# Scan stage: GpSimd also takes the product with B of step 5, eight of the 24 steps of a unit

## What is computed

```python
def _selective_scan(xs, dts, A, Bs, Cs):
    def step(h_prev, t):
        x_t, dt_t, B_t, C_t = t
        dA = jnp.exp(dt_t[..., None] * A)
        dBx = (dt_t * x_t)[..., None] * B_t[:, :, None, :]
        h = dA * h_prev + dBx
        y = jnp.einsum('bkdn,bkn->bkd', h, C_t)
        return (h, y)
    ...
    _, ys = jax.lax.scan(step, h0, seq)
```

## Time and profile before

| | before |
|---|---|
| median of 3 runs | 21461.23 us (21459.94 to 21463.92) |
| the profiled execution, its own time | 21461.03 us |
| its span, first to last instruction | 21459.2 us |
| mean granted TensorE clock | 0.785 of full speed |
| VectorE busy | 19058.9 us |
| GpSimd busy | 15280.9 us |
| TensorE matmuls busy | 16247.2 us |
| ScalarE busy | 10090.7 us |

### The profile page before, as it was taken

The page is one execution under the profiler, slowest core; times in us unless marked ns, Lnnn a source line. Parts: engine busy times, 40 slices in busy tenths (PEclk is TensorE's granted clock), DMA queues, the critical chain, the costliest instruction groups (busy, mean ns, idle before and its releaser), DMA issues. The chain is left out here.

```text
span 21459.2 us, 289980 instructions
## 1 busy us (share of the span) xinstructions
PE 16247.2 (76%) x83096; PEld 5502.1 (26%) x83096; DVE 19058.9 (89%) x21113; ACT 10090.7 (47%) x19239; POOL 15280.9 (71%) x5892
## 2 busy tenths in 40 slices
PE   8999999999977777777777777777777777777731
PEld 5555555522211111111111111111111111111111
DVE  5555555589989999999999999999999999999966
ACT  4444444467754444444444444444444444444410
POOL 0000000056669999999999999999999999999977
PEclk9999999989987777777777777777777777777755
DMA  1000000056666666666666666666666666666666
GB/s 22 18 18 18 18 18 18 18 195 226 229 196 129 127 134 131 128 132 130 129 134 131 127 132 132 129 131 131 128 133 133 127 130 133 130 131 133 127 147 166
DMA packets 1129481, 2520.46 MB, mean 117 GB/s; under 512 B 247606, under 2 KB 448824, under 8 KB 1112960
## 3 DMA queue, kind: packets, MB, share of 16 engines
q1 hardware_dynamic: 1128320, 2508.11, 52.3%
HBM read 2000.43 MB, written 507.38 MB: 117 GB/s over the span
## 5 line engine op out<-in xcount | busy, mean ns | idle before, releaser
L1235 POOL TENSOR_TENSOR c_pr<-c_hs,c_c_u 128x1568 f32<-128x1568 f32 x3072 | 9934.9, 3238 | 1037.5 <-DVE c_hs L1199 762.2
L1133 ACT ACTIVATE c_psum<-c_dt_u,c_a_neg 128x784 f32<-128x784 f32 x6144 | 5641.7, 918 | 7475.1 <-DVE c_hs L1199 7422.3
L1199 DVE TENSOR_TENSOR_SCAN c_hs<-c_psum,c_dbx 128x785 f32<-128x785 f32 (+1 forms) x4352 | 7616.3, 1773 | 20.2 <-issue 20.2
L1065 PE MATMUL c_psum<-c_pr,c_red 128*64 128x392 f32 x24576 | 7211.0, 705 | 1.0 <-POOL c_pr L1235 1.0
L1054 PE MATMUL c_psum<-c_br_u,c_sel 48*128 48x512 bf16 (+1 forms) x8704 | 2965.6, 433 | 4029.9 <-DVE c_dbx L1176 3927.8
L1176 DVE TENSOR_TENSOR c_dbx<-c_u_u,c_psum 128x784 f32<-128x784 f32 x4352 | 4103.1, 943 | 40.0 <-PE c_psum L1054 40.0
L1224 POOL TENSOR_TENSOR c_dbp<-c_u_u,c_bp_u 128x784 f32<-128x784 f32 x1792 | 3316.1, 1850 | 105.2 <-DVE c_hs L1199 62.6
L1199 DVE TENSOR_TENSOR_SCAN c_hs<-c_psum,c_dbp 128x785 f32<-128x785 f32 (+1 forms) x1792 | 3191.5, 1781 | 0.0
L196 POOL TENSOR_TENSOR a_xpb<-a_x_sb,a_pb_sb 98x768 f32<-98x768 f32 x128 | 231.2, 1807 | 4063.4 <-DVE a_x L285 4049.3
L1065 PEld LDWEIGHTS c_psum<-c_pr,c_red 128*64 128x64 f32 x24576 | 1789.8, 177 | 3404.6 <-issue 3132.1
L1054 PEld LDWEIGHTS c_psum<-c_br_u,c_sel 48*128 48x128 bf16 x8704 | 522.0, 101 | 8204.3 <-DVE c_dbx L1176 7011.4
(11 more groups left out here) (119 smaller groups left out, 17351.5 us busy)
## 6 DMA issues: line engine op xcount, KB each, us to landing
c_c_u<-scr_bc SPq DMA_DIRECT2D x512, 1568.0 KB, 28.9
c_dt_u<-scr_dt SPq DMA_DIRECT2D x512, 588.0 KB, 7.4
c_u_u<-scr_u SPq DMA_DIRECT2D x512, 588.0 KB, 11.2
c_bp_u<-scr_bc SPq DMA_DIRECT2D x512, 588.0 KB, 22.0
scr_dt<-p_dt_o SPq DMA_DIRECT2D x384, 392.0 KB, 3.0
scr_u<-p_u_o SPq DMA_DIRECT2D x384, 392.0 KB, 2.4
scr_y<-c_y_sb SPq DMA_DIRECT2D x256, 294.0 KB, 17.8
d_yin<-scr_y SPq DMA_DIRECT2D x32, 2352.0 KB, 15.5
```

The costliest lines, as they stand in the source:

```text
L1065: mm = pe.matmul(Y(3 * w + q)[64 * h:64 * h + 64, :], red[:], pr[:, s % RP, HT * h:HT * h + HT], start=(p == 0 and opens(w)), stop=(p == N ...
L1133: nc.scalar.activation(dA(s)[:, data], dt_u[:, d, s // NPR, :], ACT.Exp, scale=a_neg[:, k, s:s + 1]).then_inc(exp_done, 1)
L1199: nc.vector.tensor_tensor_scan(hs[:, s % RH, way], dA(s)[:, way], added, 0.0, ALU.mult, ALU.add).then_inc(scan_done, 1)
L1235: nc.gpsimd.tensor_tensor(pr[:, s % RP:s % RP + 2, :], hs[:, s % RH:s % RH + 2, data], c_u[:, d, s % NPR:s % NPR + 2, :], ALU.mult).then_i ...
```

## The change

Step 5 is added to `POOL_STEPS`. VectorE no longer multiplies for it, TensorE no longer spreads B for it, ScalarE writes its carried state into `dbp`. GpSimd computes it behind pair 22 of the unit before. Eight products a unit go through the ring of two, and the ring's wait moves with it: the product for step 7 now waits for scan 3, where it waited for scan 23 of the unit before; that for step 11 waits for scan 5 instead of scan 3. At the very start two products stand ahead of the first pair.

```diff
-POOL_STEPS = (3, 7, 11, 13, 15, 19, 23)
+POOL_STEPS = (3, 5, 7, 11, 13, 15, 19, 23)
...
                         if s + 7 in POOL_STEPS:
                             times_b(b, w, POOL_STEPS.index(s + 7))
-                        elif s + 7 - STEPS == POOL_STEPS[0]:
+                        elif s + 7 - STEPS in POOL_STEPS:
+                            i = POOL_STEPS.index(s + 7 - STEPS)
                             if w + 1 < WI:
-                                times_b(b, w + 1, 0)
+                                times_b(b, w + 1, i)
                             elif not last:
-                                times_b(b + 1, 0, 0)
+                                times_b(b + 1, 0, i)
 
             times_b(0, 0, 0)
+            times_b(0, 0, 1)
             images(pool, body, n_img)
```

## The result

| | before | with the change |
|---|---|---|
| median | 21461.42 us (21459.94 to 21463.92, 4 runs) | 21240.39 us (21238.69 to 21242.27, 4 runs) |
| span of the profiled execution | 21459.2 us | 21237.6 us |
| mean granted TensorE clock | 0.785 | 0.789 |

What follows compares the result with a forecast made beforehand. VectorE was taken to set the pace of the scan stage without a gap, GpSimd following. 21,461.0 less 220 us for VectorE's product, all other terms costing nothing, gave 21,241 us; range 21,220 to 21,300.

Steps and rivals of the forecast that it cites:

- What the product costs on VectorE: Scan stage: VectorE loses step 5's product in 256 units, 0.86 us each from start to start, saving 220 us.
- My line on what the profile would show: Expected signs in the profile, among them VectorE with 4,096 products instead of 4,352 and busy less by 241 us.
- GpSimd's load: Scan stage: GpSimd gains 1.81 us a unit, reaching 52.94 against a new period of 54.59, with 1.65 left.
- its base of 51.13 us a unit: GpSimd's time a unit before the change, taken from its busy time in the window, 13,088.9 / 256.
- the pass through the order: GpSimd's instructions followed once around a unit with their waits; the circle closes with 0.45 + 0.16 + 1.19 us idle.
- The order on GpSimd: GpSimd's sequence: gaps ahead of product 7 (0.5), pair 16 and pair 20 (1.2), none ahead of pairs 0 and 4.
- The spare time of VectorE's waits: VectorE's scans waiting for GpSimd: the tightest, 14 and 16, have some 3.7 us to spare, so none becomes late.
- TensorE and ScalarE: Scans 3 and 4 without a product between cost nothing; rival that either engine is late: 21,440 to 21,461 us, 3%.
- the pattern of steps 9 to 15: Existing scans there already follow each other without a product between, and VectorE does not wait: cost nothing.
- The rule on the shared port: VectorE and GpSimd share an SBUF read port; rival that GpSimd's added time holds VectorE: 21,704 us, 1%.
- GpSimd as the bound: Rival: GpSimd's 4.29 us of idle a unit can't be filled, a unit takes 57.23 us, total 21,917 us; 3%.
- The rival in which GpSimd is a little short: GpSimd instructions each 0.09 us longer would use up 1.65 us of slack a unit: 21,290 to 21,370 us; 6%.

Runs made afterwards that it cites:

- the relief alone: The changed kernel with GpSimd's product for step 5 cut to 8 of its 784 columns, output not valid: 21241.82 us, ratio 0.9897 to the kernel before.
- The load alone: The kernel before plus GpSimd's extra product of 784 columns a unit into an unread tile, VectorE keeping all 17 products: 21462.5 us, ratio 1.0.
- 392 columns more: The changed kernel plus a GpSimd product of 392 columns a unit behind pair 10, into an unread tile: 21241.75 us, ratio 0.9897 to the kernel before.
- the 784 columns: The changed kernel plus a GpSimd product of 784 columns a unit behind pair 10, into an unread tile: 21261.07 us, ratio 0.9906 to the kernel before.
- The third buffer: The changed kernel with three buffers in dbp instead of two: 21241.72 us, ratio 0.9898 to the kernel before.
- nine products: The changed kernel with step 21 also added to POOL_STEPS, nine products with B a unit on GpSimd: 21240.57 us, ratio 0.9896 to the kernel before.
- the divided product: The changed kernel with step 21's product divided, 512 columns on GpSimd and 272 on VectorE: 21130.86 us, ratio 0.9846 to the kernel before.

## Why the prediction was right

- **What the product costs on VectorE.** The term was 256 x 0.86 = 220 us from the distance between two starts. Measured: 221 for the relief alone. The whole record, 0.943, would have given 241. The same holds for busy time: the group's sum fell by 4103.1 - 3855.9 = 247 us, but the engine's busy time, in which overlaps count once, by 19058.9 - 18836.0 = 223. My line on what the profile would show said 241 for the busy time, which mixed the two up.
- **GpSimd's load.** The term of 1.81 us gave an idle of 1.65 us a unit; it is 1.71. The load alone changed nothing in the time, and 392 columns more changed nothing either. The price of the product held, but its base of 51.13 us a unit was 0.2 us too high (see the 784 columns): by distances from start to start GpSimd needs 50.95 + 1.81 = 52.76 us, and the idle to fill is 1.81, as the pass through the order also had it (0.45 + 0.16 + 1.19). With eight products that made no difference; it did where GpSimd became the bound.
- **The order on GpSimd.** The gaps ahead of product 7 and pair 20 and the lost gaps ahead of pairs 0 and 4 are as worked out in the turn shown, within 0.2 us. The third buffer shows that the new wait of product 7 costs nothing.
- **The spare time of VectorE's waits.** No scan waits for GpSimd in the changed kernel between 9000 and 19000 us. Nothing measured the 3.7 us themselves.
- **TensorE and ScalarE.** No wait of VectorE for the spread B has appeared in the stretch from 9000 to 19000 us, and the clock of the stage is 0.73 instead of 0.72. I put ScalarE at nothing by the pattern of steps 9 to 15. That holds in the change but for 1.5 us in 10,000, but the pattern was not all there was to look at: once in half an image ScalarE waits for a store of y, and I had not looked at that wait. With nine products it is 135 us.
- **The rule on the shared port.** By the advice in the Trainium skill, Perfetto Trace Analysis, section Optimizing Scalar/DVE Operations, the offload might not have helped. It helped in full. The exemption in SBUF — State Buffer, section Who interferes with whom, for VectorE instructions with at most one SBUF input (outside its two-port modes) agrees with the two runs that take the load and the relief apart: ratio 1.0 for the load alone, 221 us for the relief alone. None of the runs puts a VectorE instruction with two SBUF inputs there, so the other side of that rule is not tested here.
- **GpSimd as the bound.** It comes in at nine products, but 45 us cheaper than the sizes said, and there it costs just what VectorE gains. That both land on the same 21,240 us is chance: two engines' sums happen to agree at 54.57. The rival in which GpSimd is a little short had more room against it than I gave it, 1.8 us a unit and not 1.65.

## What to carry to other kernels

When work is moved from a full engine to one that is nearly full, price it on both by the distance from start to start, not by the records or the busy time, compare the second engine's sum with the new period, and follow the second engine's fixed order once around with its waits. If the cycle closes with some idle left and no result comes late, the move pays its whole price on the first engine, as here. Where the next whole instruction would overfill the second engine, try to divide it: between eight and nine products lay another 0.5% here.

## What the runs showed that I had not expected

- Nearly all of GpSimd's idle could be filled: with 784 more columns only 20 us of waits in 10,000 are left, although every pair waits for a scan by order. That the rings of six and eight let it lag enough is the likely reason; no run has smaller ones.
- A wait can be long in the view and cost nothing: with nine products VectorE waits 79 us for ScalarE in 10,000, while GpSimd, the bound, idles less than 2.
- ScalarE's wait for the stores of y grows, but not with the length of the unit alone. In 10,000 us it is 19.8 us before, 41.4 with eight products, 61.4 with the 784 columns on top, and 135.0 with nine, whose unit is as long as with eight; with the divided product, where the unit is shortest, it is 46.9. What grows along is the time from the issue of a store to its landing, by the median 17.8, 18.7, 19.6, 22.8 and 19.3 us in the same order. Why a store takes 4 us longer with nine products stays open.
